# A depthwise 5x5 convolution on TensorE: 24 tiles of up to 128 pixels in the place of 25 squares of 121

## The chip, the core and the metric

The kernel runs on one core of one Trainium2 chip. The metric is the device time of a launch in microseconds (us). Input and output lie in HBM in layouts that the host prepares, and that the kernel may choose.

## What is computed

The input x has 128 images of 55 by 55 pixels with 96 channels, in float32. Each channel is convolved with its own 5 by 5 taps (zero padding, same size), and x is added:

```python
k = jnp.transpose(kernel, (1, 2, 0))[:, :, None, :]
y = lax.conv_general_dilated(x, k, window_strides=(1, 1), padding='SAME', dimension_numbers=('NHWC', 'HWIO', 'NHWC'), feature_group_count=ch)
return x + y
```

## The kernel before

**Tiling.** The 96 channels are taken one after the other. The 55 by 55 plane of a channel is cut into 25 squares of 11 by 11 = 121 pixels. For one square TensorE gets the pixels of all 128 images as its stationary operand (121 pixels on the partitions, 128 images as columns), and as its moving operand a matrix that says to which outputs each pixel contributes: 121 rows, and one column for each output of the 15 by 15 window around the square (at the plane's edges 14 or 13 of a side). The result, 128 images by up to 226 outputs, is summed in PSUM. `x` is split into x_high (rounded to the format that TensorE multiplies in one pass) and x_low (the rest), the taps too, so one square costs three products: x_low by high taps, x_high by high taps, x_high by low taps. Each has its own weight load. That makes 75 products for a channel and 7200 in all (line 428).

**Sums.** Two or three squares that lie under each other share a PSUM bank: 13 sums for a channel, in turn over 8 banks. A sum may begin only when the sum eight before it has been read (`wait_bank`). ScalarE (ACT) copies 10 of the 13 sums to y_out (line 323), VectorE (DVE) copies the other three (354) and adds the seams, four rows (357) or columns (363) wide, in which neighbouring sums overlap.

**Preparing a channel.** x arrives by a DMA of 1.6 MB on SyncE's queue (SP), four channels ahead. ACT makes x_high (315) in two pieces, DVE makes x_low of the first piece, and GpSimd (POOL) x_low of the second (254). POOL also builds the moving operand: `place_taps` (249) multiplies the five turned rows of taps with a mask; the split of the taps for four channels at a time (lines 233, 235, 237) stands in POOL's queue too. weights, x_high and x_low have two slots each, so a channel is prepared while the one before it is multiplied. All queues are written out by hand and each engine takes its own in order.

**Waits.** TensorE (PE) waits for `weights_ready` once a channel, for x_low once a piece, and for the bank of each sum. SP stores a channel (1.5 MB, line 278) when its last seam is added, and behind that store it issues the next load of x.

**Start.** PE first multiplies zeros, 17 products of 512 columns, while the first channel comes in five pieces. The first taps are split and placed by DVE.

Of the kernel before, what the change touches and what calls it, by code (L numbers as in the profile page):

```python
# [14 lines left out]
HALO = TAPS // 2  # L15
P = 128

# [4 lines left out]
SIDE = 11  # L22
GRID = HEIGHT // SIDE
SQUARE = SIDE * SIDE
WINDOW = SIDE + 2 * HALO
SQUARES = GRID * GRID
STRIP_COLS = GRID * IMAGES
X_COLS = SQUARES * IMAGES


TAP_COLS = WINDOW * WINDOW
TAP_AT = 16
PART_COLS = TAP_AT + WINDOW * (WINDOW + 1)
HIGH, LOW = range(2)
# [4 lines left out]
REPEATS = WINDOW // TAPS  # L39
TURNED_COLS = TAPS * WINDOW  # L40
assert WINDOW % TAPS == 0
# [3 lines left out]


EDGE = WINDOW - 1
SUM_COLS = ((1, EDGE),) + ((0, WINDOW),) * (GRID - 2) + ((0, EDGE),)

SEAM = 2 * HALO  # L50
FRESH = tuple(min(WIDTH, SIDE * (j + 1) + HALO) - (SIDE * j + HALO if j else 0) for j in range(GRID))
FRESH_AT = (1,) + (SEAM,) * (GRID - 1)
Y_AT = tuple(HEIGHT * sum(FRESH[:j]) for j in range(GRID + 1))
assert Y_AT[-1] == HEIGHT * WIDTH
Y_COLS = 3072

TILES = tuple((j, squares) for j in range(GRID) for squares in (
    ((0, 1), (2, 3, 4)) if SUM_COLS[j][1] == EDGE else ((0, 1), (2, 3), (4,))))  # L60


def first_row(square):
    return max(0, SIDE * square - HALO)


def end_row(square):
    return min(HEIGHT, SIDE * (square + 1) + HALO)


def tile_rows(tile):
    squares = TILES[tile][1]
    return first_row(squares[0]), end_row(squares[-1])
# [4 lines left out]
def copied_by_act(tile):  # L78
    return len(TILES[tile][1]) > 1


def row_seam(tile):
    return TILES[tile][1][0] > 0


def col_seam(tile):
    return TILES[tile][0] > 0
# [3 lines left out]
COPIES = [sum(copied_by_act(n) for n in range(i + 1)) for i in range(len(TILES))]  # L91
STEPS = [sum((not copied_by_act(n)) + row_seam(n) + col_seam(n) for n in range(i + 1)) for i in range(len(TILES))]
# [5 lines left out]

BATCH = 4
BATCHES = CHANNELS // BATCH  # L100
BATCHES_AHEAD = 2
TAPS_SLOTS = 4
SPLIT_SLOTS = 2
SPLIT_STEPS = 3
ZERO_COLS = 512
ZERO_PRODUCTS = 17


FIRST_PIECES = tuple((j, j + 1) for j in range(GRID))
LATER_PIECES = ((0, 2), (2, GRID))  # L110


def pieces_of(c):
    return FIRST_PIECES if c == 0 else LATER_PIECES

# [6 lines left out]
def uses(c, slots):  # L122

    return c // slots
# [374 lines left out]
```

## Time and profile before

| | |
|---|---|
| median of 3 runs | 821.78 us (820.1 to 821.82) |
| profiled execution: its own time, its span | 820.36 us, 818.6 us |
| PE products; weight loads | 811.2 us busy; 809.2 us |
| ACT, POOL, DVE | 617.4 us (75%), 620.6 us (76%), 538.9 us (66%) |
| DMA | 313.40 MB, mean 383 GB/s |

The span runs from the first to the last instruction. The share of busy time of an engine says how full it is, not whether anything waits for it; for that the chain of waits and the waits of each engine are read. The recorded duration of a product includes its way through the array, so products overlap in the record; their pace is read from the distance between their starts.

### The profile page before, as it was taken

Reading aid. Unit: us, or ns where it says so; the run is one execution under the profiler, and the core shown is the slowest. Engines: PE = TensorE matmul, PEld = TensorE weight load, DVE = VectorE, ACT = ScalarE, POOL = GpSimd, SP = SyncE. Lnnn points to the kernel's source line nnn. Section 1 sums busy time; section 2 is a strip of 40 time slices with the busy share of each in tenths; the row PEclk is TensorE's granted clock in tenths of the full one; section 3 lists DMA queues with packets and bytes.
Section 4 is the critical chain, followed back from the end, with each engine's and each line's share of the span. In section 5 each row is a group of like instructions: output and inputs, shape, how many; then the busy total and the mean of one; then the engine's idle time right before and its main releaser. Section 6 shows DMA issues by size and latency. Waiting matters only on the chain.

```text
span 818.6 us, 19694 instructions
## 1 busy us (share of the span) xinstructions
PE 811.2 (99%) x7217; PEld 809.2 (99%) x7217; DVE 538.9 (66%) x2224; ACT 617.4 (75%) x1157; POOL 620.6 (76%) x263
## 2 busy tenths in 40 slices
PE   8999999999999999999999999999999999999997
PEld 7999999999999999999999999999999999999997
DVE  6666666666666666666666666666666666666664
ACT  6777777777777777777777777777777777777774
POOL 2978878778696786977778878778696786977772
PEclk9999999999999999999999999999999999999999
DMA  9999999999999999999999999999999999999965
GB/s 370 418 414 393 388 387 386 392 385 396 395 389 393 375 402 388 387 391 383 395 391 391 389 386 386 395 381 395 395 387 394 380 399 381 390 390 391 389 246 232
DMA packets 32497, 313.40 MB, mean 383 GB/s; under 512 B 3600, under 2 KB 6800, under 8 KB 8080
## 3 DMA queue, kind: packets, MB, share of 16 engines
q1 hardware_dynamic: 31968, 311.67, 97.4%
q8 instruction: 57, 0.93, 0.4%
q10 hardware_dynamic: 432, 0.46, 0.2%
q14 instruction: 40, 0.33, 0.1%
HBM read 161.13 MB, written 150.99 MB: 381 GB/s over the span
## 4 chain that ended last, share of the span: by engine, by line
PE 98%; DMA 1%; DVE 0%; ACT 0%; ACTq 0%; issue 0%; DVEq 0%
PE sums L428 98%; DMA places_in<-places 1%; DVE x_low L254 0%; DVE weights L249 0%; DVE rest L235 0%; DVE taps_split L233 0%; DVE taps_split L237 0%; ACT y_out L323 0%; ACTq L219 0%; DVEq L163 0%; DVE y_out L357 0%; DVEq L228 0%
## 5 line engine op out<-in xcount | busy, mean ns | idle before, releaser
L428 PE MATMUL sums<-weights,x_high 121*128 121x226 f32 (+3 forms) x4800 | 804.1, 274 | 0.0
L428 PEld LDWEIGHTS sums<-weights,x_high 121*128 121x128 f32 x4800 | 729.0, 192 | 0.0
L428 PE MATMUL sums<-weights,x_low 121*128 121x226 f32 (+3 forms) x2400 | 659.1, 275 | 1.5 <-DVE x_low L254 1.5
L254 POOL TENSOR_TENSOR x_low<-x_in,x_high 121x1920 fp32r<-121x1920 f32 x95 | 411.9, 4336 | 175.3 <-ACT x_high L315 175.3
L323 ACT ACTIVATE y_out<-sums 128x264 f32<-128x264 f32 (+2 forms) x960 | 360.4, 398 | 189.8 <-PE sums L428 176.0
L428 PEld LDWEIGHTS sums<-weights,x_low 121*128 121x128 f32 x2400 | 460.8, 192 | 1.9 <-issue 1.9
L363 DVE TENSOR_TENSOR y_out<-sums,y_out 128x96 f32<-128x96 f32 (+3 forms) x1056 | 263.0, 249 | 123.3 <-ACT y_out L323 102.3
L315 ACT ACTIVATE x_high<-x_in 121x1920 fp32r<-121x1920 f32 (+1 forms) x195 | 295.2, 1514 | 5.3 <-DMA x_in<-x 5.2
L254 DVE TENSOR_TENSOR x_low<-x_in,x_high 121x1280 fp32r<-121x1280 f32 (+1 forms) x100 | 170.1, 1704 | 71.1 <-ACT x_high L315 71.1
L357 DVE TENSOR_TENSOR y_out<-sums,y_out 128x44 f32<-128x44 f32 (+2 forms) x768 | 152.0, 198 | 76.6 <-ACT y_out L323 76.3
L249 POOL TENSOR_TENSOR weights<-taps_split,places_in 121x450 fp32r<-121x450 f32 x95 | 133.7, 1407 | 7.2 <-DVE taps_split L237 7.2
L354 DVE COPY y_out<-sums 128x99 f32<-128x99 f32 x288 | 72.5, 252 | 0.7 <-PE sums L428 0.3
L235 POOL TENSOR_TENSOR rest<-taps_split,places_in 121x300 f32<-121x300 f32 x23 | 43.8, 1905 | 1.8
L237 POOL TENSOR_TENSOR taps_split<-taps_in,rest 121x300 fp32r<-121x300 f32 x23 | 19.3, 838 | 1.8
L233 POOL TENSOR_TENSOR taps_split<-taps_in,places_in 121x300 fp32r<-121x300 f32 x23 | 17.8, 775 | 0.0
L436 PE MATMUL sums<-zeros 128*128 128x512 f32 x17 | 6.9, 588 | 1.5 <-DVE zeros L365 1.5
L436 PEld LDWEIGHTS sums<-zeros 128*128 128x128 f32 x17 | 5.1, 308 | 2.8 <-DVE zeros L365 1.4
L329 ACT ACT_TABLE_LOAD x1 | 1.3, 1283 | 2.1 <-issue 2.1
L233 DVE TENSOR_TENSOR taps_split<-taps_in,places_in 121x300 fp32r<-121x300 f32 x1 | 0.5, 473 | 3.3 <-DMA places_in<-places 3.3
L365 DVE MEMSET zeros<- 128x512 f32 x1 | 0.5, 485 | 0.9 <-PEq L492 0.9
L368 DVE MEMSET weights<- 128x512 f32 x2 | 1.0, 485 | 0.1
L249 DVE TENSOR_TENSOR weights<-taps_split,places_in 121x450 fp32r<-121x450 f32 x1 | 0.6, 628 | 0.0
(9 smaller groups left out, 1.9 us busy)
## 6 DMA issues: line engine op xcount, KB each, us to landing
x_in<-x SPq DMA_DIRECT2D x95, 1600.0 KB, 11.6
y<-y_out SPq DMA_DIRECT2D x95, 1536.0 KB, 7.5
taps_in<-taps SPq DMA_DIRECT2D x22, 150.0 KB, 11.8
x_in<-x SPq DMA_DIRECT2D x5, 320.0 KB, 5.3
y<-y_out SPq DMA_DIRECT2D x3, 302.5 KB, 2.5
y<-y_out SPq DMA_DIRECT2D x1, 357.5 KB, 3.7
taps_in<-taps ACTq DMA_DIRECT2D x2, 150.0 KB, 4.9
y<-y_out SPq DMA_DIRECT2D x1, 271.0 KB, 2.6
```

Source lines behind the costliest of these rows:

```text
L233: engine.tensor_tensor(high, given, centre, ALU.add).then_inc(taps_step, 1)
L235: engine.tensor_tensor(left, high.bitcast(F32), centre, ALU.subtract).then_inc(taps_step, 1)
L237: engine.tensor_tensor(low, given, left, ALU.subtract).then_inc(taps_step, 1)
L249: engine.tensor_tensor(windows, turned, mask, ALU.mult).then_inc(weights_ready[slot], 1)
L254: engine.tensor_tensor(x_low[slot][0:SQUARE, cols], x_in[c % X_SLOTS][0:SQUARE, cols], x_high[slot][0:SQUARE, cols].bitcast(F32), ALU.subt ...
L315: act.activation(x_high[c % SLOTS][0:SQUARE, cols], x_in[c % X_SLOTS][0:SQUARE, cols], ACT.Copy).then_inc(high_ready[c % SLOTS], 1)
L323: act.activation(y, sums, ACT.Copy).then_inc(tile_copied, 1)
L354: dve.tensor_copy(*fresh(c, i)).then_inc(y_step, 1)
L357: dve.tensor_tensor(seam, sums[:, 0:SEAM, FRESH_AT[j]:FRESH_AT[j] + FRESH[j]], seam, ALU.add).then_inc(y_step, 1)
L363: dve.tensor_tensor(seam, sums[:, :, 0:SEAM], seam, ALU.add).then_inc(y_step, 1)
L428: product = pe.matmul(sums, v[slot][0:SQUARE, at:at + IMAGES], window, start=n == 0 and v is x_low, stop=n == len(squares) - 1 and part == ...
L436: pe.matmul(psum[:, 0, :], zeros[:, 0:P], zeros[:, :], start=True, stop=True)
```

## The change

The plane of a channel is cut into 24 tiles: three bands of seven blocks, 16 rows by 8 columns = 128 pixels (the seventh has 7 columns), then a foot of three tiles, 7 rows by 18 columns = 126 pixels. The seven pixels in the last column of the foot are in no tile: their contribution to 9 by 3 outputs is computed on DVE for groups of 12 channels (`sum_corner`, twelve small steps for a group, one in a channel; the first group, of four channels, on POOL before everything else there) and added to the plane of each channel.

A channel has 72 products in 12 sums, 6912 products in all. A window is 12 columns wide and 20 rows high in the second and third band, 18 high in the first; a sum now holds tiles that lie beside each other, so that a product writes rows of 10 or 12 with the pitch of the sum, and no longer one run. x has 3072 columns for a channel (3200 before). y_out is one plane with rows of 55, before it was five strips.

There are two moving operands to place for a channel, for the blocks (128 by 480, one instruction) and for the foot (126 by 225, two instructions), both by POOL. The split of the taps (420 columns for four channels, 300 before) moves from POOL's queue to DVE's, one of its three steps in each of three channels. ACT copies 10 of the 12 sums, DVE two. The first channel comes in other pieces, and DVE makes x_low for three of its five pieces and POOL for two; before, DVE made all. ACT's queue loads 0.55 MB at the start (first taps, centre, mask), 0.12 MB and 1.08 MB (corner), before two taps' batches and 0.15 MB. 14 products of zeros instead of 17.

```diff
+BLOCK_H, BLOCK_W = 16, 8
+BANDS = 3
+STRIPS = 7
+FOOT = BLOCK_H * BANDS
+FOOT_H, FOOT_W = HEIGHT - FOOT, 18
+FOOT_TILES = 3
+FOOT_PIXELS = FOOT_H * FOOT_W
+CORNER_COL = FOOT_W * FOOT_TILES
+assert CORNER_COL == WIDTH - 1
+TILES = BANDS * STRIPS + FOOT_TILES
+X_COLS = TILES * IMAGES
...
+GROUPS = ((0, 4), (4, 12)) + tuple((c, c + 12) for c in range(12, CHANNELS, 12))
+CORNER_STEPS = 2 + 2 * TAPS
...
+SUMS = ((0, (0, 1, 2)), (0, (3, 4)), (0, (5, 6)),
+        (1, (0, 1)), (1, (2, 3)), (1, (4, 5)), (1, (6,)),
+        (2, (0, 1)), (2, (2, 3)), (2, (4, 5)), (2, (6,)),
+        (BANDS, (0, 1, 2)))
...
+def pitch_of(i):
+    first, end = cols_of(i)
+    return end - first + (end - first) % 2
...
+def copied_by_act(i):
+    return i not in (6, 10)
...
-ZERO_PRODUCTS = 17
+ZERO_PRODUCTS = 14
+
+
+FIRST_PIECES = ((0, 3), (3, 7), (7, 14), (14, 21), (21, 24))
+LATER_PIECES = ((0, 11), (11, 24))
...
-    return c == 0 or piece == 0
+    return piece < 3 if c == 0 else piece == 0
...
+        def place_block(engine, c):
+            shape = [P, 2, REPEATS, BLOCK_TURNED]
+            at = c % BATCH * BLOCK_TURNED
+            turned = taps_split[c // BATCH % SPLIT_SLOTS][:, :, at:at + BLOCK_TURNED].bitcast(F32)
+            mask = block_mask.rearrange("p (a n) -> p a n", n=BLOCK_TURNED)
+            windows = block_weights[c % SLOTS][:, :, :].rearrange("p w (a n) -> p w a n", n=BLOCK_TURNED)
+            engine.tensor_tensor(windows, turned.unsqueeze(2).broadcast_to(shape),
+                                 mask.unsqueeze(1).broadcast_to(shape), ALU.mult).then_inc(block_ready[c % SLOTS], 1)
...
+        def place_foot(engine, c):
+            shape = [FOOT_PIXELS, FOOT_ROWS, FOOT_REPEATS, TAPS]
+            at = BATCH * BLOCK_TURNED + c % BATCH * FOOT_TURNED
+            mask = foot_mask[0:FOOT_PIXELS, :].rearrange("p (u b n) -> p u b n", b=FOOT_REPEATS, n=TAPS)
+            for part in (HIGH, LOW):
+                turned = taps_split[c // BATCH % SPLIT_SLOTS][0:FOOT_PIXELS, part, at:at + FOOT_TURNED].bitcast(F32)
+                turned = turned.rearrange("p (u n) -> p u n", n=TAPS).unsqueeze(2).broadcast_to(shape)
+                window = foot_weights[c % SLOTS][0:FOOT_PIXELS, part, :, 0:FOOT_REPEATS * TAPS].rearrange(
+                    "p u (b n) -> p u b n", n=TAPS)
+                engine.tensor_tensor(window, turned, mask, ALU.mult).then_inc(foot_ready[c % SLOTS], 1)
...
+        def sum_corner(engine, group, step):
...
+            engine.wait_ge(corner_step[group > 0], CORNER_STEPS * max(0, group - 1) + step)
+            if step == CORNER_STEPS - 1:
+                own = sums[:, :, HALO:HALO + FOOT_H, HALO]
+                engine.tensor_tensor(own, pixels, own, ALU.add).then_inc(corner_step[group > 0], 1)
+                return
...
+            if adds:
+                to = sums[:, :, row:end_row, :]
+                engine.tensor_tensor(to, part, to, ALU.add).then_inc(corner_step[group > 0], 1)
+            else:
...
+                engine.tensor_tensor(part, pixels[:, :, row + shift:end_row + shift].unsqueeze(3).broadcast_to(shape),
+                                     rows.unsqueeze(2).broadcast_to(shape), ALU.mult).then_inc(corner_step[group > 0], 1)
...
-            load_taps(act, 0)
-            act.dma_start(places_in[:, :], places).then_inc(places_loaded, 16)
+            act.dma_start(start_in[:, :], start).then_inc(start_loaded, 16)
+            act.dma_start(foot_mask[:, :], foot).then_inc(foot_loaded, 16)
+            act.dma_start(corner_in[:, :], corner).then_inc(corner_loaded, 16)
...
+                if col_seam(i):
+                    seam = y[:, row + down:end_row, col:col + SEAM]
+                    dve.tensor_tensor(seam, sums[:, down:, 0:SEAM], seam, ALU.add).then_inc(y_step, 1)
+                if i == LAST_SUM:
+                    dve.wait_ge(y_step, stepped(c, i) - 1)
+                    group = group_of(c)
+                    dve.wait_ge(corner_step[group > 0], CORNER_STEPS * max(1, group))
+                    part = corner_sum[group % GROUP_SLOTS][:, c - GROUPS[group][0], :, :]
+                    seam = y[:, HEIGHT - CORNER_ROWS:HEIGHT, WIDTH - CORNER_OUT:WIDTH]
+                    dve.tensor_tensor(seam, part, seam, ALU.add).then_inc(y_step, 1)
 
...
+                todo = []
+                group = group_of(c)
+                first, end = GROUPS[group]
+                if group + 1 < len(GROUPS):
+                    share = [CORNER_STEPS * (n - first) // (end - first) for n in (c, c + 1)]
+                    todo = list(range(*share))
+                if c // BATCH + 1 < BATCHES and c % BATCH < SPLIT_STEPS:
+                    split_taps(dve, c // BATCH + 1, c % BATCH)
...
+                    if i in (5, 8, 11) and todo:
+                        sum_corner(dve, group + 1, todo.pop(0))
...
-            for c in range(1, CHANNELS):
-                place_taps(pool, c)
-                split_low(pool, c, 1, low_by_pool)
-                if c % BATCH == BATCH // 2 and c // BATCH + 1 < BATCHES:
-                    split_taps(pool, c // BATCH + 1)
+            pool.wait_ge(start_loaded, 16)
+            pool.wait_ge(corner_loaded, 16)
+            for step in range(CORNER_STEPS):
+                sum_corner(pool, 0, step)
+            pool.wait_ge(foot_loaded, 16)
+            for c in range(CHANNELS):
+                wait_split(pool, c)
+                if c > 0:
+                    place_block(pool, c)
+                place_foot(pool, c)
+                for piece in range(len(pieces_of(c))):
+                    if not by_dve(c, piece):
+                        split_low(pool, c, piece, low_by_pool)
 
...
+                    sums = sum_view(c, i)[:, :, to:to + right - left]
+                        if foot_tile:
+                            window = foot_weights[slot][0:pixels, part, :, left:right]
...
+                            window = block_weights[slot][:, part, :].rearrange("p (r c) -> p r c", c=WINDOW_W)[
+                                :, above:above + end - first, left:right]
```

What stands in the queues, at three places.

POOL in the middle of the program before: one batch of four channels (`weights` is the moving operand, `rest` and `taps_split` the split of the taps).

```order
L249 TENSOR_TENSOR weights<-taps_split,places_in 121x2x225
L254 TENSOR_TENSOR x_low<-x_in,x_high 121x1920
L233 TENSOR_TENSOR taps_split<-taps_in,places_in 121x4x75
L235 TENSOR_TENSOR rest<-taps_split,places_in 121x300
L237 TENSOR_TENSOR taps_split<-taps_in,rest 121x4x75
L249 TENSOR_TENSOR weights<-taps_split,places_in 121x2x225
```

POOL at its beginning now (from the last steps of the corner to the second channel; `foot_weights` and `block_weights` are the two moving operands).

```order
L347 TENSOR_TENSOR corner_part<-corner_in 128x84
L341 TENSOR_TENSOR corner_sum0<-corner_part,corner_sum0 128x4x21
L332 TENSOR_TENSOR corner_sum0<-corner_in,corner_sum0 128x4x7
L306 TENSOR_TENSOR foot_weights0<-taps_split0,foot_mask 126x9x25 x2
L311 TENSOR_TENSOR x_low0<-x_in0,x_high0 128x896
L311 TENSOR_TENSOR x_low0<-x_in0,x_high0 128x384
L294 TENSOR_TENSOR block_weights1<-taps_split0,start_in 128x480
L306 TENSOR_TENSOR foot_weights1<-taps_split0,foot_mask 126x9x25 x2
L311 TENSOR_TENSOR x_low1<-x_in1,x_high1 128x1664
```

The split of the taps has left POOL; the corner of the first group now stands ahead of x_low of the first channel, and each later channel is one block, two feet and one x_low.

DVE now, in the first part of a channel in the middle (the step at line 280 is the third of a split, that at 347 a step of the corner; 448 and 453 are the seams).

```order
L311 TENSOR_TENSOR x_low<-x_in,x_high 128x1408
L280 TENSOR_TENSOR taps_split<-taps_in,rest 128x420
L448 TENSOR_TENSOR y_out<-sums,y_out 128x18x4 x2
L453 TENSOR_TENSOR y_out<-sums,y_out 128x4x18
L448 TENSOR_TENSOR y_out<-sums,y_out 128x16x4
L453 TENSOR_TENSOR y_out<-sums,y_out 128x4x20
L448 TENSOR_TENSOR y_out<-sums,y_out 128x16x4
L453 TENSOR_TENSOR y_out<-sums,y_out 128x4x20
L347 TENSOR_TENSOR corner_part<-corner_in 128x252
L445 COPY y_out<-sums 128x16x5
```

Before, the same stretch had no split and no corner:

```order
L254 TENSOR_TENSOR x_low<-x_in,x_high 121x1280
L357 TENSOR_TENSOR y_out<-sums,y_out 128x52
L363 TENSOR_TENSOR y_out<-sums,y_out 128x24x4
L357 TENSOR_TENSOR y_out<-sums,y_out 128x44
L363 TENSOR_TENSOR y_out<-sums,y_out 128x26x4
L354 COPY y_out<-sums 128x99
```

A step of the split (in three channels of four) now stands between x_low and the seams, and a step of the corner between them.

PE before, three squares inside the plane (121 rows by 226 outputs in one run), and now, three blocks of the second band (20 rows of 12 outputs, with the pitch of the sum).

```order
L428 MATMUL sums<-weights,x_low 128x226
L428 MATMUL sums<-weights,x_high 128x226 x2
L428 MATMUL sums<-weights,x_low 128x226
L428 MATMUL sums<-weights,x_high 128x226 x2
L428 MATMUL sums<-weights,x_low 128x196
```

```order
L542 MATMUL sums<-block_weights,x_low 128x20x12
L542 MATMUL sums<-block_weights,x_high 128x20x12 x2
L542 MATMUL sums<-block_weights,x_low 128x20x12
L542 MATMUL sums<-block_weights,x_high 128x20x12 x2
L542 MATMUL sums<-block_weights,x_low 128x200
```

A tile keeps its three products; a product has up to 240 columns where it had up to 226.

## Rows read from the trace of the kernel before

**Rows 1.** The page, part 1: engine, busy us (share of the span) xinstructions.
```profile
PE 811.2 (99%) x7217; PEld 809.2 (99%) x7217; DVE 538.9 (66%) x2224; ACT 617.4 (75%) x1157; POOL 620.6 (76%) x263
```

**Rows 2.** Chain of work that ended last: start us, us, what.
```profile
1.17 4.73 DMA places_in<-places
...
5.98 0.48 DVE taps_split L233
...
7.50 0.63 DVE weights L249
8.13 1.59 DVE x_low L254
9.72 0.14 issue
9.85 804.28 PE sums L428 x7200
```

**Rows 3.** Timeline of PE mid-program: start us, us, instruction.
```profile
403.58 0.27 PE L428 MATMUL sums<-weights,x_low 121*128 121x182 f32 x1
...
403.92 0.29 PE L428 MATMUL sums<-weights,x_low 121*128 121x210 f32 x1
...
405.26 0.27 PE L428 MATMUL sums<-weights,x_low 121*128 121x196 f32 x1
...
405.59 0.28 PE L428 MATMUL sums<-weights,x_low 121*128 121x226 f32 x1
...
405.94 0.27 PE L428 MATMUL sums<-weights,x_low 121*128 121x226 f32 x1
```

**Rows 4.** Timeline of PE's zero products: all, the last three, the last two.
```profile
1.45 6.90 PE L436 MATMUL sums<-zeros 128*128 128x512 f32 x17 [1.45 <-DVE zeros L365]
...
7.49 0.86 PE L436 MATMUL sums<-zeros 128*128 128x512 f32 x3
...
7.72 0.63 PE L436 MATMUL sums<-zeros 128*128 128x512 f32 x2
```

**Rows 5.** Groups by form: count | busy us, mean ns | idle before, releaser.
```profile
L254 POOL TENSOR_TENSOR x_low<-x_in,x_high 121x1920 fp32r<-121x1920 f32 x95 | 411.9, 4336 | 175.3 <-ACT x_high L315 175.3
...
L249 POOL TENSOR_TENSOR weights<-taps_split,places_in 121x450 fp32r<-121x450 f32 x95 | 133.7, 1407 | 7.2 <-DVE taps_split L237 7.2
...
L323 ACT ACTIVATE y_out<-sums 128x242 f32<-128x242 f32 x288 | 108.0, 375 | 52.8 <-PE sums L428 52.8
...
L323 ACT ACTIVATE y_out<-sums 128x403 f32<-128x403 f32 x96 | 49.0, 510 | 0.6 <-PE sums L428 0.6
L235 POOL TENSOR_TENSOR rest<-taps_split,places_in 121x300 f32<-121x300 f32 x23 | 43.8, 1905 | 1.8
...
L237 POOL TENSOR_TENSOR taps_split<-taps_in,rest 121x300 fp32r<-121x300 f32 x23 | 19.3, 838 | 1.8
```

**Rows 6.** POOL's instructions of line 249: ns min/median/max, first and last start.
```profile
L249 POOL TENSOR_TENSOR weights<-taps_split,places_in x95: 1034/1092/2422, 7.6 to 798.5; 121x450 fp32r<-121x450 f32 x95
```

**Rows 7.** Groups by form of ACT's and DVE's other work, as rows 5.
```profile
L315 ACT ACTIVATE x_high<-x_in 121x1920 fp32r<-121x1920 f32 x95 | 171.1, 1801 | 0.0
L254 DVE TENSOR_TENSOR x_low<-x_in,x_high 121x1280 fp32r<-121x1280 f32 x95 | 165.5, 1742 | 71.1 <-ACT x_high L315 71.1
...
L357 DVE TENSOR_TENSOR y_out<-sums,y_out 128x44 f32<-128x44 f32 x576 | 113.9, 198 | 1.5 <-ACT y_out L323 1.2
...
L363 DVE TENSOR_TENSOR y_out<-sums,y_out 128x96 f32<-128x96 f32 x384 | 100.0, 260 | 123.3 <-ACT y_out L323 102.3 <-DVE y_out L357 0.5
```

**Rows 8.** Windows: us, busy of each engine (x), granted clock, DMA share, GB/s.
```profile
36.00:56.00 20.00, 20.00 (x182) 20.00 (x181) 13.37 (x51) 15.71 (x30) 14.05 (x6) 1.00 1.01 424
400.00:420.00 20.00, 20.00 (x181) 20.00 (x180) 13.10 (x59) 14.98 (x30) 15.84 (x7) 1.00 1.00 381
420.00:440.00 20.00, 20.00 (x182) 20.00 (x180) 12.88 (x50) 15.46 (x29) 16.88 (x9) 1.00 1.00 396
...
816.00:818.00 2.00, 0.00 (x0) 0.00 (x0) 0.00 (x0) 0.00 (x0) 0.00 (x0) 0.58 0.72 277
```

**Rows 9.** DMA issues: count, KB each, median us to landing.
```profile
x_in<-x SPq DMA_DIRECT2D x95, 1600.0 KB, 11.6
```

More of the change, by code:

```diff
@@ L93, with row_seam, col_seam @@
+def copied_by_act(i):
+    return i not in (6, 10)
+def row_seam(i):
+    return SUMS[i][0] > 0
+def col_seam(i):
+    return SUMS[i][1][0] > 0
+LAST_SUM = len(SUMS) - 1
+COPIES = [sum(copied_by_act(n) for n in range(i + 1)) for i in range(len(SUMS))]
+STEPS = [sum((not copied_by_act(n)) + row_seam(n) + col_seam(n) + (n == LAST_SUM) for n in range(i + 1))
+         for i in range(len(SUMS))]
 COPIES_ALL, STEPS_ALL = COPIES[-1], STEPS[-1]
@@ L152, in bank_of, with group_of, build @@
 def bank_of(c, i):
-    return (c * len(TILES) + i) % BANKS
-LAST_TILE = len(TILES) - 1
+    return (c * len(SUMS) + i) % BANKS
+def group_of(c):
+    return next(g for g, (first, end) in enumerate(GROUPS) if first <= c < end)
 LAST = CHANNELS - 1
-LAST_STORES = tuple((Y_AT[j], Y_AT[j + 1] if j < GRID - 1 else Y_COLS) for j in range(GRID))
-def build(nc, x, taps, places, out):
+LAST_STORES = ((6, 0, WIDTH * (2 * BLOCK_H - HALO)),
+               (10, WIDTH * (2 * BLOCK_H - HALO), WIDTH * (FOOT - HALO)),
+               (11, WIDTH * (FOOT - HALO), Y_COLS))
+def build(nc, x, taps, start, foot, corner, out):
     with ExitStack() as ctx:
@@ L443, in _ @@
                     pe.wait_ge(low_ready[slot], lows(c, piece))
[L444 to L446 removed]
+                    for i in range(len(SUMS)):
+                        if first <= tiles_of(i)[0] < end:
+                            sum_tiles(c, i)
 def lay_out_input(x):
[L450 to L451 removed]
@@ new lines, in lay_out_masks, with lay_out_corner @@
+def lay_out_masks():
+    block = np.zeros((P, WINDOW_H, WINDOW_W), np.float32)
+    for r in range(BLOCK_H):
+        block[r * BLOCK_W:(r + 1) * BLOCK_W, r:r + TAPS] = 1
+    foot = np.zeros((P, FOOT_ROWS, FOOT_REPEATS * TAPS), np.float32)
+    for c in range(FOOT_W):
+        foot[c:FOOT_PIXELS:FOOT_W, :, c:c + TAPS] = 1
+    return block.reshape(P, -1), foot.reshape(P, -1)
+def lay_out_corner(x, taps):
+    pixels = x[:, FOOT:, CORNER_COL, :].transpose(0, 2, 1).reshape(P, -1)
+    reach = taps[:, :, :HALO - 1:-1].reshape(1, -1)
+    return np.concatenate([pixels, np.repeat(reach, P, axis=0)], axis=1)
```

378 lines of the change are left out of this document (191 added, 187 removed).

## The prediction

> **What bounds the kernel now.** I read the page's shares of busy time first: PE and its weight loads stand at 99%, ACT, POOL and DVE at 66 to 76% [rows 1]. A busy share alone doesn't say that an engine sets the end, so the chain of waits comes next. It is one piece: 804.28 us of products in a row, from 9.85 on, no wait between them [rows 2]. Only the start (9.85 us) and the tail (818.6 - 814.1 = 4.5 us) lie outside. So the question is what sets the pace of a product: 804.28 / 7200 = 111.7 ns.
>
> The timeline answers it. A product of x_low begins a tile of three. From 403.58 to 403.92 (182 columns) are 0.34 us, from 403.92 to 405.26 (nine products of 210 columns, three of 182) 1.34 us or 111.7 ns each, from 405.26 to 405.59 (196) 0.33 us, from 405.59 to 405.94 (226) 0.35 us [rows 3]. At 2.4 GHz a column takes 0.417 ns, so 182 columns would need 76 ns and 226 94 ns: the pace follows the products and not their columns. What every product has alike is one load of 128 weight columns. A load has 268 cycles of 2.4 GHz here. PE is therefore bound by the number of products, and columns are free as long as a product streams in less than 111.7 ns.
>
> **What the change does, part by part.**
>
> *Products.* 75 become 72 for a channel, 7200 become 6912: 6912 x 111.7 = 772.1 us, 32.2 less. Columns rise from 15,594 to 15,648 for a channel, which costs nothing by the pace above. One form is new in size: 240 columns, in five tiles of each of two bands, 30 products a channel, 2880 in all. They stream in 100 ns, 11.7 under the pace. Bounds: from below nothing is gained (the load stays). From above the last zero products have 512 columns and start 0.23 us apart, where 213 ns are 512 columns, so some 17 to 20 ns lie between two long products [rows 4]; a product of 240 columns would take up to 120 ns, 8.3 more, 24 us in all. I take nothing: with 20 ns on top, the 2592 products of 226 columns would need 114 ns and the mean of all products would be 112.6, not the 111.7 that the stretch of 210 columns has. But 226 leaves 17.5 ns free and 240 only 11.7, and the writes to PSUM now go in rows of 10 or 12, so I keep the 24 us.
>
> The stationary operand has 128 rows of pixels instead of 121. The trace has no paced load of 128 rows: the nearest is the load of 121 rows. If the time went by rows, it were 111.7 x 128/121 = 118.2 ns. The 268 cycles are 2.09 for each of 128 columns, near a whole number, and 2.21 for each row; I take no change. The Trainium skill (TensorE: Matmul & The Clock Gate, section LDWEIGHTS (loading the stationary operand)) says that a load takes P/1.2 ns with P the columns, whatever the rows: 106.7 ns for 128. By that rule the term stays 772, by rows it would be 815; the trace has 5 ns more than the rule.
>
> *POOL, for each channel.* x_low of 13 tiles is 1664 columns where 1920 took 4336 ns, 2.26 ns each [rows 5]: 3.76 us. The block window is 480 columns; 450 took 1407 ns on average, 3.13 each, but 1034 in the fastest and 2422 in the slowest [rows 6]: 1.50 us (1.1 to 2.6). The foot is 2 x 225 columns in runs of five. No row has such runs; the nearest by size are 838 ns for 300 columns (2.8 each) and 1905 for 300 (6.35 each) [rows 5]: 1.26 us, up to 2.86. The sum is 6.5 us, between 6.1 and 9.2, against 72 x 111.7 = 8.04 us in which PE now does a channel. POOL's share rises from 76 to some 81% though the split of the taps leaves it. What counts is when x_low of the second piece is there: PE wants it after 11 tiles, 3.7 us into the channel, and waits for nothing as long as POOL's channel is under 8.04 us. That leaves 8.04 - 3.76 = 4.28 us for 930 columns, 4.6 ns each. I stay with the cheaper rows.
>
> *ACT.* Ten copies stay ten; their columns rise from 2728 to 2865. 242 columns take 375 ns and 403 take 510 [rows 5], 0.84 ns a column: 0.1 us more. x_high loses 128 columns of 3200, 0.1 us less [rows 7]. ACT keeps its 6.4 us a channel, 80% of 8.04.
>
> *DVE.* 538.9 / 96 = 5.6 us a channel now [rows 1]. x_low grows from 1280 to 1408 columns, by a tenth of 1742 ns [rows 7]: 0.2. A channel has 18 seams and two copies, and one corner add, for 22 operations before, about the same (198 to 260 ns each, overlapping [rows 7]). The split adds 0.6 us in three of four channels, a corner step some 0.4 to 0.5 us in each: 0.9 on average. Sum 6.6 us, 82% of 8.04. Behind these steps the seams of a channel are queued, and for them PE's bank waits: a sum wants the bank of the one eight before, 5.4 us earlier. x_high and x_low of the next channel come first (3.7 us from the channel's start), then the split and the seams of the first five sums, to about 5.2 us; the first such bank is wanted at 6.0. It is close and I count nothing; without that cover it costs tenths of a us a channel.
>
> *DMA.* A channel moved 1.64 + 1.57 + 0.04 = 3.25 MB in 8.38 us, 388 GB/s. Now it is 1.57 + 1.57 + 0.05 = 3.20 MB in 8.04 us, 398 GB/s. The DMA share is 1.00 throughout, at 381 to 396 GB/s; but for 20 us, right after the start, the same mix ran at 424 [rows 8], and a load lands after 11.6 us [rows 9] of the three channels (25 us) it has. So 398 is within reach. The Trainium skill (HBM Reference, section Specifications (TRN2)) gives a core 358 GB/s as its share when both cores of the domain run, and some 425 to one alone; by the first figure 309 MB would take 862 us, and the trace is already above it (383 on average).
>
> *Start.* Before, PE begins at 9.85: taps and mask land 4.73 us after their issue, three splits of 0.48, placing 0.63, x_low 1.59 [rows 2]. Now 0.55 MB has to land for 0.31 (0.6 us at 424 GB/s), the splits have 420 columns for 300 (0.5 in all), the first piece of x_low 384 for 640 (0.5 less): 10.4. Then POOL. It waits for 1.08 MB of the corner, behind 0.67 MB on ACT's queue and beside 1.6 MB of x: 3.3 MB at 424 GB/s are 7.8 us, there at about 10. The corner has 904 columns, 2.5 to 5.7 us at 2.8 to 6.35 ns; the feet 1.3 to 2.9; x_low of 896 columns 2.0. PE wants that after 42 products, at 15.1, and it is there at 15.8 to 20.6: 0.7 to 5.5 us of waiting, I take 3. PE's clock: the first 14 zero products took 6.04 us or 431 ns each, which is 1.2 GHz, and the next 0.23 [rows 4]; after the last product at 814.1 the granted clock is 0.58 in the window from 816 on [rows 8]. With three zero products fewer PE idles from 7.6 to 10.4, and again in the wait for POOL. Another slow stretch like the first costs half of its 6 us: I take 3, with bounds 0 and 6.
>
> *Tail.* As before, plus one add for the corner: 4.8 us.
>
> **Sum.** 10.4 + 772.1 + 3 + 3 + 4.8 = 793.3 us of span. The profiled execution's own time is 820.36 for a span of 818.6, 1.8 more; the median of the runs is 821.78, another 1.4: 796.5, say **797 us**. With the start's bounds alone 791 to 803.
>
> **The rivals.**
> (a) *POOL becomes the bound, and the kernel slower.* If the short runs of the foot and the block window cost what the slow rows cost (6.35 and 5.4 ns a column), POOL's channel is 3.76 + 2.6 + 2.86 + 0.15 for gaps = 9.4 us; 95 x 9.4 + 22 for the first channel + 8 for the end and the difference of times = 923 us. It decides from 4.6 ns a column on. For it: the slow rows exist (a mean of 1407 over a median of 1092 means that about one placing in four is slow [rows 6]), and these windows have more and shorter runs. Against: the median placing is 1092 ns, 2.4 a column. With slow feet alone POOL takes 8.3 us and the time is about 818.
> (b) *The wide products set their own pace*, 120 ns: 797 + 24 = 821, in a weaker form 809.
> (c) *The DMA is at its end at 388 GB/s*, as its share of 1.00 says: 3.20 MB take 8.24 us a channel, 95 x 8.24 + 30 = 813. Against it stands the 424.
> (d) *Loads go by rows*: 815.4 in place of 772.1, 840 us.
> (e) *The seams come late for the banks* on DVE's longer queue: 0.1 us a channel, 807.
>
> **Chances.** The forecast 0.58; (a) 0.10 in full and 0.05 in half; (b) 0.13; (c) 0.07; (d) 0.03; (e) 0.04. About 0.2% (1.6 us) is what a measurement of this kernel tells from no change. Faster: 0.58 and the half of (a), most of (b), (c) and (e), 0.84; same: the upper end of (b), 0.03; slower: (a) in full and (d), 0.13. The range reaches from 786 (no waits at the start, no slow clock, a shorter tail) to 820; it leaves out (a), (d) and a bit of the rest.
>
> **What would show it.** Right: the 6912 products take 111.7 ns each also where they have 240 columns; PE waits once for x_low by POOL before 22 us and hardly after. Wrong: starts 118 to 120 ns apart in the second and third band (b) or everywhere (d); waits of PE for POOL's x_low in every channel, with feet over 1.3 us each (a); ACT waiting for x to land and loads landing after 20 us or more (c); waits of PE for DVE's seams (e).

## The result, and the profile after

The changed kernel took **854.38 us** (median of 4 runs, 853.85 to 856.42) against 821.06 of the kernel before in the same job: a ratio of 1.0411, with a 95% interval of 1.0389 to 1.0433. It is slower; 797 was forecast. The profiled execution has a span of 852.9 us, where the sum of the prediction was 793.3.

The page's part 1 of the kernel after, columns as in [rows 1]:

```profile
PE 806.1 (95%) x6926; PEld 789.8 (93%) x6926; DVE 780.4 (91%) x2193; ACT 613.9 (72%) x1157; POOL 635.1 (74%) x400
```

PE lost its 99%. DVE went from 538.9 to 780.4 us, 2.5 us more a channel where I had 1.0, with fewer instructions than before (2193 for 2224). So something on DVE became long. The groups by form (count | busy us, mean ns of one | idle before, releaser) say what:

```profile
L347 DVE TENSOR_TENSOR corner_part<-corner_in 128x252 f32<-128x252 f32 x21 | 66.4, 3163 | 0.0
L341 DVE TENSOR_TENSOR corner_sum<-corner_part,corner_sum 128x252 f32<-128x252 f32 x21 | 64.9, 3091 | 0.0
...
L332 DVE TENSOR_TENSOR corner_sum<-corner_in,corner_sum 128x84 f32<-128x84 f32 x7 | 20.7, 2951 | 0.0
```

A corner step of 252 columns takes 3.1 us, and one of 84 columns nearly as long: the time isn't made of columns. The timeline (start us, us, instruction) shows what it is made of; two stretches of DVE, then the one of POOL beside the second:

```profile
37.09 0.30 DVE L347 TENSOR_TENSOR corner_part<-corner_in 128x144 f32<-128x144 f32 x1
...
402.79 0.23 DVE L453 TENSOR_TENSOR y_out<-sums,y_out 128x80 f32<-128x80 f32 x1
402.94 3.52 DVE L347 TENSOR_TENSOR corner_part<-corner_in 128x252 f32<-128x252 f32 x1
406.38 0.23 DVE L445 COPY y_out<-sums 128x80 f32<-128x80 f32 x1
...
402.41 3.77 POOL L311 TENSOR_TENSOR x_low<-x_in,x_high 128x1664 fp32r<-128x1664 f32 x1 [2.42 <-ACT x_high L406]
```

POOL's x_low runs from 402.41 to 406.18. DVE's corner step begins 0.5 us after it and ends at 406.46, 0.28 us after it. The seam just ahead of it, at 402.79, also lies beside x_low and takes its 0.23 us. The step at 37.09, with POOL idle, takes 0.30. So the step does no work for 3.2 us: it stands still until POOL is done. It is the rule and not the exception: of the 88 steps on DVE, 76 begin while POOL's x_low runs, and each of them ends 0.14 to 0.29 us behind it. Every seam behind such a step in DVE's queue stands too, and PE, which wants the banks that the seams read, waits for them. PE's waits (us in total, times, longest):

```profile
PE sums L542 <- DVE y_out L453: 30.0, 75, 0.5
PE sums L542 <- POOL x_low L311: 4.8, 1, 4.8
PE sums L542 <- DVE y_out L448: 4.2, 1, 4.2
PE sums L542 <- DVE x_low L311: 2.6, 2, 2.0
```

What else the prediction asked of the profile is there as forecast. The groups of POOL by form:

```profile
L311 POOL TENSOR_TENSOR x_low<-x_in,x_high 128x1664 fp32r<-128x1664 f32 x95 | 358.8, 3777 | 191.1 <-ACT x_high L406 190.4
...
L306 POOL TENSOR_TENSOR foot_weights<-taps_split,foot_mask 126x225 fp32r<-126x225 f32 x192 | 148.4, 794 | 0.0
L294 POOL TENSOR_TENSOR block_weights<-taps_split,start_in 128x480 fp32r<-128x480 f32 x95 | 127.1, 1338 | 5.0 <-PE sums L542 5.0
```

x_low 3.78 us (3.76 forecast), a foot 0.79 (0.63), the blocks 1.34 (1.50): 6.7 us a channel, far from rival (a). The last twelve channels have no corner steps, and there, from 753.88 us on, PE is never idle. Windows, columns as in [rows 8]:

```profile
400.00:420.00 20.00, 19.11 (x168) 18.75 (x168) 19.11 (x50) 14.99 (x28) 12.76 (x9) 1.00 0.96 367
...
780.00:800.00 20.00, 20.00 (x181) 20.00 (x180) 16.66 (x59) 15.85 (x31) 19.27 (x11) 1.00 1.01 423
```

From 753.88 us on 849 products start within 95.04 us, 112.1 ns apart; products of 240 columns are among them and start 0.34 us apart by threes like the others. That refutes rival (b), wide products, and (d), loads by rows. The DMA moves 423 GB/s there, which refutes (c). The 367 GB/s of the middle are what a slower channel asks for, not a limit.

### The profile page after: what moved, and what is told of

The parts are those of the page before. It is cut to its first block, busy times and chain, and to the rows that moved or that the text cites. A ratio compares the mean times of both kernels' runs of the same rounds, so it can differ in the third digit from the quotient of the medians.

```text
span 852.9 us, 19211 instructions
## 1 busy us (share of the span) xinstructions
PE 806.1 (95%) x6926; PEld 789.8 (93%) x6926; DVE 780.4 (91%) x2193; ACT 613.9 (72%) x1157; POOL 635.1 (74%) x400
## 2 busy tenths in 40 slices
DMA packets 32351, 309.93 MB, mean 363 GB/s; under 512 B 3584, under 2 KB 6912, under 8 KB 7808
## 4 chain that ended last, share of the span: by engine, by line
DVE 52%; PE 38%; issue 3%; ACT 3%; DMA 1%; POOL 1%; SPq 0%; DVEq 0%; ACTq 0%
PE sums L542 38%; DVE corner_sum L341 13%; DVE corner_part L347 11%; DVE x_low L311 9%; DVE y_out L453 7%; DVE y_out L448 5%; DVE corner_sum L332 2%; ACT y_out L414 2%; DVE y_out L445 2%; DMA x_in<-x 1%; ACT x_high L406 1%; DVE taps_split L280 1%; DVE rest L277 1%; DVE y_out L460 1%; DVE taps_split L274 1%
## 5 line engine op out<-in xcount | busy, mean ns | idle before, releaser
L542 PE MATMUL sums<-block_weights,x_high 128*128 128x240 f32 (+3 forms) x4032 | 691.6, 276 | 0.0
L542 PEld LDWEIGHTS sums<-block_weights,x_high 128*128 128x128 f32 x4032 | 613.3, 192 | 0.0
L542 PE MATMUL sums<-block_weights,x_low 128*128 128x240 f32 (+3 forms) x2016 | 565.8, 281 | 41.6 <-DVE y_out L453 30.0
L414 ACT ACTIVATE y_out<-sums 128x256 f32<-128x256 f32 (+3 forms) x960 | 368.0, 418 | 224.8 <-PE sums L542 224.6
L311 POOL TENSOR_TENSOR x_low<-x_in,x_high 128x1664 fp32r<-128x1664 f32 (+1 forms) x97 | 363.3, 3745 | 191.1 <-ACT x_high L406 190.4
L542 PEld LDWEIGHTS sums<-block_weights,x_low 128*128 128x128 f32 x2016 | 386.4, 192 | 56.8 <-DVE y_out L453 43.5
L406 ACT ACTIVATE x_high<-x_in 128x1664 fp32r<-128x1664 f32 (+1 forms) x195 | 284.2, 1458 | 7.8 <-DMA x_in<-x 7.8
L453 DVE TENSOR_TENSOR y_out<-sums,y_out 128x80 f32<-128x80 f32 (+3 forms) x864 | 206.8, 239 | 38.2 <-ACT y_out L414 9.5
L311 DVE TENSOR_TENSOR x_low<-x_in,x_high 128x1408 fp32r<-128x1408 f32 (+2 forms) x98 | 169.9, 1734 | 11.7 <-ACT x_high L406 11.7
L448 DVE TENSOR_TENSOR y_out<-sums,y_out 128x64 f32<-128x64 f32 (+1 forms) x768 | 160.2, 219 | 11.5 <-ACT y_out L414 9.0
L347 DVE TENSOR_TENSOR corner_part<-corner_in 128x252 f32<-128x252 f32 (+5 forms) x40 | 122.7, 3067 | 0.0
L341 DVE TENSOR_TENSOR corner_sum<-corner_part,corner_sum 128x252 f32<-128x252 f32 (+5 forms) x40 | 111.7, 2792 | 0.0
L460 DVE TENSOR_TENSOR y_out<-corner_sum,y_out 128x27 f32<-128x27 f32 x96 | 25.2, 262 | 3.3
```

The source lines that it names most:

```text
L311: engine.tensor_tensor(x_low[slot][:, cols], x_in[c % X_SLOTS][:, cols], x_high[slot][:, cols].bitcast(F32), ALU.subtract).then_inc(low_re ...
L341: engine.tensor_tensor(to, part, to, ALU.add).then_inc(corner_step[group > 0], 1)
L347: engine.tensor_tensor(part, pixels[:, :, row + shift:end_row + shift].unsqueeze(3).broadcast_to(shape), rows.unsqueeze(2).broadcast_to(sh ...
L406: act.activation(x_high[c % SLOTS][:, cols], x_in[c % X_SLOTS][:, cols], ACT.Copy).then_inc(high_ready[c % SLOTS], 1)
L414: act.activation(y, sums, ACT.Copy).then_inc(tile_copied, 1)
L448: dve.tensor_tensor(seam, sums[:, down:, 0:SEAM], seam, ALU.add).then_inc(y_step, 1)
```

## The experiments

Each ratio is to the kernel before in the same job, which had 820.2 to 822.0 us. "Period" is the mean time from a channel's first product to the next channel's, over channels 8 to 80; before it is 8.375 us, after 8.671, and 72 products at 111.7 ns would be 8.04. "Start" is the same for channels 0 to 2 together: 25.2 before, 40.8 after.

**Is it the corner at all?** *no_corner* takes the steps and the corner's add out; its output lacks the seven pixels' contributions. *memset_steps* leaves them in their places, but from the second group on each is a memset of what it would write; the corner's values are then zeros.

```diff
-                    if i in (5, 8, 11) and todo:
-                        sum_corner(dve, group + 1, todo.pop(0))
...
```
```diff
...
+            if group:
+                engine.memset(sums[:, :, row:end_row, :] if adds else part, 0.0).then_inc(corner_step[1], 1)
```

> The changed kernel without anything of the corner: no steps of it on DVE or POOL, and no add of it (seven pixels' contributions are left out). Theory W (DVE's corner steps, two inputs from SBUF each, stand still while POOL's x_low of 3.8 us runs, and hold up the seams and so PE's banks): PE hardly waits after the start, a channel takes 8.04 us, and with the start's wait for POOL shorter the time is 787 to 796. Rival R (DVE's queue is too long with the split of the taps and x_low even without the corner, or the DMA is at its end): a channel stays above 8.3 us, 815 or more.

> The changed kernel with every corner step after the first group replaced by a memset of the same output, in the same place on DVE (no inputs; the corner's values from channel 4 on are left out). Theory W: a memset has no input from SBUF and does not wait for POOL: 0.3 us each, a channel of 8.04 us, 792 to 806. Rival P (any instruction on DVE in that place, or writing SBUF beside POOL, is held up, or the mere place in the queue costs): 3 us each and 845 to 860.

Measured 797.35 us for no_corner (ratio 0.971, interval 0.9688 to 0.9733; 1.4 us above its range) and 797.35 for memset_steps (0.9712, 0.9692 to 0.9732). Both have a period of 8.061. The corner costs 57 us, and all of it goes when the instructions stay in place, in number and in output, and write a constant in the place of reading SBUF and adding or multiplying. A memset of 252 columns takes:

```profile
L343 DVE MEMSET corner_part<- 128x252 f32 x21 | 5.6, 268 | 0.0
```

So it isn't the number of instructions in the queue, nor a semaphore, nor the write.

**The same thing made in the kernel before.** *probe_in_before* puts one add of 252 columns from two SBUF tensors behind the seams of sum 5 of each channel; *probe_copy* a copy of 252 columns; *probe_reduce* a sum of neighbours (252 columns read, 126 written).

```diff
...
+                    if i == 5:
+                        dve.wait_ge(probe_step, 2 + c)
+                        dve.tensor_tensor(probe[0][:, :], probe[1][:, :], probe[2][:, :], ALU.add).then_inc(probe_step, 1)
```

> The kernel before with one more instruction a channel: DVE adds two SBUF tensors of 252 contiguous columns (a probe that nothing uses) behind the seams of the sixth sum, where POOL's x_low of 4.34 us runs. Theory W (a DVE operation with two inputs from SBUF stands still until POOL's x_low ends): the add takes 2.5 to 4 us instead of 0.4, DVE's 5.6 us a channel grow to 8.5 to 9.5 against 8.38, PE waits for seams, and the time is 850 to 920. Rival Q (the changed kernel's DVE is only too full, its steps slow by their strides): 0.4 us, and 820 to 824.

> The kernel before with one more DVE instruction a channel, in the place of probe_in_before's 252-column add: a copy of as many columns from SBUF to SBUF, one input, float32. Theory (only an instruction of DVE with two SBUF inputs stands still beside POOL's x_low): the copy takes 0.2 to 0.4 us and the kernel 820 to 824. Rival (DVE's instruction stops by whatever it does in SBUF, or a one-input copy takes POOL's port as well): the copy takes 3 to 4 us, ends with POOL's x_low, and the kernel comes to 900 to 950, like probe_in_before (951.9).

> The kernel before with one DVE instruction more a channel, in the place of probe_copy's copy: it reads the same 252 columns from SBUF and writes the 126 sums of two neighbours. By the Trainium skill (SBUF - State Buffer, section Who interferes with whom) a copy between SBUF tensors can take POOL's pair of ports, a reduction on this chip never does. Theory (the DVE instruction stops only if it needs POOL's ports, by a second SBUF input or as a copy that reads through both): the reduction takes 0.2 to 0.5 us and the kernel 820 to 824. Rival (any DVE instruction whose inputs are all in SBUF stops): it takes 3 to 4 us and the kernel 930 to 950, like probe_copy (938.9).

Measured 951.85 us (ratio 1.1595, 1.1573 to 1.1616), 938.9 (1.1421, 1.1392 to 1.145) and 820.61 (1.0001, 0.999 to 1.0012). The groups of the three probes, one of each kernel:

```profile
L388 DVE TENSOR_TENSOR probe<-probe 128x252 f32<-128x252 f32 x96 | 384.2, 4002 | 0.0
```
```profile
L388 DVE COPY probe<-probe 128x252 f32<-128x252 f32 x96 | 370.6, 3860 | 0.0
```
```profile
L388 DVE TENSOR_REDUCE probe<-probe 128x126 f32<-128x252 f32 x96 | 38.9, 406 | 0.0
```

One small add a channel costs this kernel 131 us, more than the 30 to 100 that I expected; 95 of the 96 adds end 0.27 to 0.28 us behind POOL's x_low, and the one that doesn't meet it takes 0.41 us. My own theory for the copy (only two inputs stop) was refuted: a copy stops as well, 95 of the 96, and ends 0.15 us behind x_low (0.28 us where it meets none). The reduction, with its input in SBUF too, doesn't; it lies inside POOL's x_low in the timeline and takes 0.41 us:

```profile
362.28 0.41 DVE L388 TENSOR_REDUCE probe<-probe 128x126 f32<-128x252 f32 x1
...
361.88 4.33 POOL L256 TENSOR_TENSOR x_low<-x_in,x_high 121x1920 fp32r<-121x1920 f32 x1 [3.00 <-ACT x_high L317]
```

This is the rule of the Trainium skill (SBUF — State Buffer, section Who interferes with whom): DVE and POOL share one pair of SBUF ports, and it is a lock held for a whole instruction, not a bandwidth. DVE needs it for a second SBUF input or when a copy reads through both ports; a reduction on this chip never does. By that rule and these runs seams (one input in PSUM) and memsets are free, as the trace has them.

**Where the steps stand.** *corner_early* puts them behind the split of the taps, before a channel's first seam; *corner_late* behind its last seam; *corner_on_pool* gives them to POOL, behind its x_low.

```diff
                 for i in range(len(SUMS)):
                     finish_sums(c, i)
-                    if i in (5, 8, 11) and todo:
-                        sum_corner(dve, group + 1, todo.pop(0))
+                for step in todo:
+                    sum_corner(dve, group + 1, step)
```

> The changed kernel with the same corner steps on DVE, only placed directly behind the split of the taps at the channel's beginning, before the first seam, where POOL waits for x_high. Theory W: a step takes about 0.3 us instead of 3.1, a channel 8.04 us, the time is 790 to 803 (the start stays as it is, 10 to 15 us of loss). Rival S (the steps are slow by themselves, by runs of three elements and strides): they take 3 us here too, and the time stays at 845 to 860.

> The changed kernel with the corner steps of a channel on DVE behind its last seam, where DVE waits 0.9 us a channel for x_high in the run without a corner, and POOL places the block. Theory W extended (V: DVE's and POOL's instructions with two SBUF inputs share one supply, their times add up, and with the corner it is POOL whose channel passes 8.04 us): steps of 0.3 to 0.9 us, POOL's channel 8.1 to 8.25 us as in the early placing, 803 to 820. If only x_low's standing still counted (W alone): 795 to 802.

> The changed kernel with all later corner steps moved from DVE to POOL, behind its x_low of the channel. Theory W: POOL takes 0.6 to 0.9 us for a step of 252 columns, its channel rises from 6.4 to some 7.2 us, under 8.04; DVE's seams are no longer held up; 792 to 806. Rival S: slow runs cost on POOL too (3 us), POOL's channel passes 9 us, 870 or more.

Measured:

| kernel | us, ratio (interval) | period | start | a 252-column step (L347) |
|---|---|---|---|---|
| corner_early | 819.1, 0.9984 (0.9972 to 0.9996) | 8.149 | 40.7 | 0.86 us |
| corner_late | 809.66, 0.9853 (0.9814 to 0.9892) | 8.150 | 40.6 | 1.12 us |
| corner_on_pool | 823.28, 1.0027 (1.0016 to 1.0039) | 8.336 | 34.4 | 0.70 us, on POOL |

The diff is that of corner_late. The same instructions, moved in one queue, win back 45 us there: none of the 88 begins beside x_low, they meet POOL's blocks and feet (0.6 to 1.3 us long). corner_early's trace is 21.3 us longer than no_corner's: 9.7 of it lie in the start, 5.7 in channel 5, which took 13.7 us because a step of 3.80 us just met x_low and held the seams, and some 7 are spread over the others. That expectation (790 to 803) was missed, and so was corner_on_pool's (792 to 806). On POOL a step costs no more than it does beside short instructions, but POOL is now busy for 97% of the span (94% in no_corner), its own standing counted: its block takes 2.30 us on average where it takes 1.23 in no_corner. PE waits 36 times for DVE's seams, 10.1 us in all. corner_late's time is inside its range (803 to 820). DVE and then POOL, two stretches of one timeline of corner_on_pool:

```profile
355.67 1.52 DVE L460 TENSOR_TENSOR y_out<-corner_sum,y_out 128x27 f32<-128x27 f32 x1
357.11 2.09 DVE L311 TENSOR_TENSOR x_low<-x_in,x_high 128x1408 fp32r<-128x1408 f32 x1
359.13 1.61 DVE L274 TENSOR_TENSOR taps_split<-taps_in,start_in 128x420 fp32r<-128x420 f32 x1
...
357.09 0.64 POOL L341 TENSOR_TENSOR corner_sum<-corner_part,corner_sum 128x216 f32<-128x216 f32 x1
357.67 2.62 POOL L294 TENSOR_TENSOR block_weights<-taps_split,start_in 128x480 fp32r<-128x480 f32 x1
360.25 1.62 POOL L306 TENSOR_TENSOR foot_weights<-taps_split,foot_mask 126x225 fp32r<-126x225 f32 x2
```

The shortest records of their forms are 1.61 and 0.59 us for DVE's x_low and split, 1.21 and 2 x 0.62 for POOL's block and feet, 4.7 in all, and with POOL's step ahead of them (0.64) some 5.3; side by side they needed 4.8 (357.09 to 361.87). So in this stretch about nine tenths of their times add up as if the two were one engine. The corner's add of 27 columns, with two inputs in SBUF as well, takes 1.52 us beside POOL's x_low, and 0.19 where it meets nothing.

**More work from POOL to DVE.** *late_dve14* is corner_late with 14 tiles of x_low on DVE; *late_dve14_start* also moves the first group's steps from POOL to DVE.

```diff
-LATER_PIECES = ((0, 11), (11, 24))
+LATER_PIECES = ((0, 14), (14, 24))
```

> As corner_late, and the boundary between DVE's and POOL's x_low moves from tile 11 to tile 14: DVE takes 1792 columns, POOL 1280. Theory V: a column costs DVE 1.15 ns and POOL 2.26, so the shared supply is used 0.43 us less a channel and POOL's channel falls to some 7.3 us: PE hardly waits after the start, 790 to 803. If DVE's length is what counts (its channel grows by 0.44 us to 6.8 or more): 815 to 830.

> As late_dve14, and the corner of the first group is computed by DVE behind its pieces of x_low of channel 0, no longer by POOL ahead of everything. Theory V: POOL starts x_low of channel 0 some 5 us earlier, PE's wait of 4.8 us near 14 us goes, with it most of the slow clock behind it: 5 to 12 us less than late_dve14, 784 to 795. If the start is bound by the landing of x: no difference.

Measured 812.26 us (0.9894, 0.9879 to 0.9909; period 8.206) and 813.43 (0.991, 0.9896 to 0.9925), both missed. POOL's share fell to 71% and DVE's rose to 91%, yet the channel got 0.06 us longer. My theory had the sum of both engines' SBUF work as the bound, and by its prices that sum fell by 0.43 us a channel (384 columns, 2.26 - 1.15 ns each). So the sum alone doesn't set the pace here. POOL sat idle for 215 us before its x_low, for want of x_high; the few waits that PE's rows show from 60 to 780 us (4, 1.1 us in all) are for DVE's seams. DVE's in-order queue is then the likelier bound, but no run separates the two. The start of late_dve14 is shorter, 35.2 us for the 40.6 of corner_late.

**One late step.** *start_and_balanced* is start_reordered (below) with a group's corner steps collected in every fourth channel, where no taps are split.

> start_reordered with the corner steps of a group of four channels put into its fourth channel alone, where no taps are split (in group 0 three steps a channel). Theory: the lost time of 0.09 us a channel of corner_late is the corner steps and the taps' split together in one channel of DVE; apart, the period comes to 8.07 to 8.10 us, 4 to 6 us less than start_reordered: 791 to 799. Rival (what is lost is each corner step's time beside POOL, wherever it stands): the mean period stays at 8.13 to 8.16 and the time within 2 us of start_reordered; or four times as many steps in one channel fill it past 8.05 us and the period is above 8.16.

Measured 926.62 us (four runs, 918.07 to 936.39; the ratio, 1.1238, interval 1.1171 to 1.1306, is that of the three up to 929.32), 128 us above the upper end of its range. The trace is of the execution of 936.39. DVE, then POOL:

```profile
134.59 0.42 DVE L347 TENSOR_TENSOR corner_part<-corner_in 128x252 f32<-128x252 f32 x1
135.04 0.42 DVE L341 TENSOR_TENSOR corner_sum<-corner_part,corner_sum 128x252 f32<-128x252 f32 x1
135.50 0.30 DVE L332 TENSOR_TENSOR corner_sum<-corner_in,corner_sum 128x84 f32<-128x84 f32 x1
135.70 1.63 DVE L311 TENSOR_TENSOR x_low<-x_in,x_high 128x1408 fp32r<-128x1408 f32 x1
137.23 4.09 DVE L274 TENSOR_TENSOR taps_split<-taps_in,start_in 128x420 fp32r<-128x420 f32 x1
...
135.79 5.08 POOL L311 TENSOR_TENSOR x_low<-x_in,x_high 128x1664 fp32r<-128x1664 f32 x1 [1.53 <-ACT x_high L408]
```

The steps make DVE's x_low late, it meets POOL's x_low, and now POOL is the one that waits (5.08 us for 3.77); the split behind it then waits for POOL (4.09 for 0.59), and PE waits 5.4 us for the seams. Whichever starts first holds the ports. PE waited so 22 times, 81.9 us in all, and most of these channels took 14 to 15 us. The granted clock adds to it: 1.00 from 120 to 135 us and 0.77 from 135 to 150, where PE waited 5.4.

**The start.** *start_reordered* is corner_late with ACT's copies and DVE's first seams of channel 0 before x_high and x_low of channel 1, the first group's corner steps on DVE before channel 0's last seam, and the corner's load on SP's queue. *corner_inside_start* has these steps between the seams of sums 3 and 4, the second group's in channels 1 to 3, and the corner's load on ACT's queue behind the second taps. The diff, against the changed kernel, is of the latter:

```diff
...
+                early = range(5) if c == 0 else ()
+                for i in early:
+                    finish_sums(c, i)
+                    if i == 3:
+                        dve.wait_ge(corner_loaded, 16)
+                        for step in range(CORNER_STEPS):
+                            sum_corner(dve, 0, step)
...
```

> Corner steps behind the last seam of a channel, as in corner_late (809.7 us), and the first channels reordered: ACT copies channel 0's sums before it makes x_high(1), DVE adds the seams of channel 0's sums 0 to 4 before it makes x_low(1), the first group's corner steps stand on DVE just before the last sum's seam, and POOL starts with the feet. Theory (DVE's and POOL's instructions with two SBUF inputs stop each other, and the queue behind them is what PE waits for): the periods of channels 8 to 95 stay at 8.13 to 8.16 us, and of the start's 9 us beyond 8.05 in channel 0 and some 6 in channel 1 some 8 to 12 come back: 797 to 803. Rival (the start's loss is the first loads from HBM and the cold clock, not the order of DVE, ACT and POOL): channel 0 keeps 16 to 17 us and the time stays at 808 to 811.

> start_reordered with the first group's corner steps between the seams of channel 0's sums 3 and 4, where DVE waits for x_high of channel 1 (10.7 to 16.1 us), and the second group's in channels 1 to 3. Theory (in start_reordered corner steps beside POOL's x_low of channel 2 held the seams until 31 us, a wait of 5.7 us for PE and then a slow clock until 41 us): channels 0 to 2 take 27 to 32 us together where they took 40.6, and the kernel 797 to 802. Rival (the start costs the same wherever the corner steps stand, by the loads from HBM or the clock): 38 to 41 us and 808 to 811.

Measured 810.1 us (0.986, 0.9832 to 0.9889) and 807.24 (0.9868, 0.981 to 0.9927; its runs reach from 804.5 to 815.4, so the two are not told apart by their times). The traces tell more. In start_reordered channel 0 fell from 17.1 to 9.7 us, but channel 1 rose from 14.4 to 20.6: two of the first group's steps met x_low (3.7 and 3.6 us), PE waited 5.7 us, and the granted clock of 31.4 to 39.4 was 0.50, which is 1.2 GHz, where 14 to 22 had 1.00. The forecast of 797 to 803 was missed: the time is the rival's (808 to 811), though channel 0 fell as the theory had it. In corner_inside_start channels 0 to 2 take 32.4 us in place of 40.6, just outside the 27 to 32 expected, and the period stays at 8.142; its time, too, lies above the expected 797 to 802. Its PE waits:

```profile
PE sums L553 <- DVE x_low L311: 6.6, 2, 3.7
PE sums L561 <- DVE zeros L464: 1.5, 1, 1.5
PE sums L553 <- DVE y_out L450: 1.1, 5, 0.3
```

corner_late, start_reordered and corner_inside_start are the fastest complete kernels of this study, 1.3 to 1.5% faster than before and not told apart from each other. Above no_corner, the traces of the first and the last have 7.9 and 7.5 us from channel 3 on, some 0.08 us a channel, and 9.5 and 1.3 in the start.

## Why the prediction was wrong

The predicted span was 793.3 and the measured one 852.9, 59.6 us more. By the steps of the prediction:

- **Products: right.** 112.1 ns each where nothing waits (8.061 / 72 = 112.0 in no_corner), 240 columns and 128 rows included: 0.3 ns above the 111.7 of the sum, 2 us in all.
- **POOL: right** in its rows (6.7 us a channel, 6.5 forecast), and in no_corner and memset_steps PE waits for it nowhere behind the first channel. But rival (a) priced it by rows that were themselves waits, as told below.
- **ACT, DMA: right.** ACT 6.4 us a channel; 423 GB/s reached when asked for.
- **DVE: the step that failed.** "a corner step some 0.4 to 0.5 us": the price holds for a step that meets nobody (0.30 us for 144 columns, 0.42 for 252 in start_and_balanced), but beside x_low it takes 3.1. The overlap was wrong: a step on DVE and POOL's x_low were taken to run side by side, and they don't. "It is close and I count nothing; without that cover it costs tenths of a us a channel": this cover was not there. From channel 3 to the end of the last product the trace after has 799.8 us, where 93 channels of 8.04 are 747.9: 51.9 us of the 59.6. In memset_steps the same stretch has 749.9, so 49.9 of the 51.9 are the steps' standing and 2.0 the pace of the products. The symptom had been named as rival (e), seams late for the banks, at 0.1 us a channel and a chance of 0.04; it took 0.6 in the middle channels (8.671 - 8.04). The stop behind it had not been named: the nearest rows were those of the seams [rows 7], whose one input lies in PSUM. No row of before showed a short instruction with two SBUF inputs on DVE beside POOL's x_low. memset_steps shows that the cost lies in what the step reads and computes and not in its place, number or writes; probe_in_before and the ends of its adds behind x_low show the standing still without the rest of the change. (The count of seams was off as well, 17 a channel and not 18, which changes nothing.)
- **The start: mis-sized, for the most part by the same step.** Channels 0 to 2 took 40.8 us, for 24.1 of products and 6 of waits and slow clock allowed: 10.7 more. PE waited 4.8 us for x_low by POOL, inside the 0.7 to 5.5 given, and 4.2 more for seams behind the taps' split, which itself stood 4.1 us beside POOL's x_low; then the clock was 0.76 in 20 to 40 us. The split met x_low because a corner step ahead of it had stood 3.89 us (from 24.15 on): in memset_steps the split is done before POOL's x_low begins, the wait of 4.2 us is gone, and the start takes 33.5 us. So 7.3 of the 10.7 are the corner's too, and 3.4 remain. First product at 8.57 for 10.4 (1.8 less), and a tail of 3.7 for 4.8 (1.1 less). 51.9 + 10.7 - 1.8 - 1.1 = 59.7.

The corner step, the split and POOL's x_low beside the split, in the start of the changed kernel:

```profile
24.15 3.89 DVE L347 TENSOR_TENSOR corner_part<-corner_in 128x120 f32<-128x120 f32 x1
...
31.91 4.08 DVE L277 TENSOR_TENSOR rest<-taps_split,start_in 128x420 f32<-128x420 f32 x1
...
31.66 3.88 POOL L311 TENSOR_TENSOR x_low<-x_in,x_high 128x1664 fp32r<-128x1664 f32 x1 [1.35 <-ACT x_high L406]
```

The trace of before had a sign that I read wrongly. POOL's line 249 had 1034 ns at least and 2422 at most [rows 6], and I took the long ones for a matter of runs in memory. They are those that lie beside DVE's x_low. All 24 of over 2.3 us share 1.39 to 1.46 us with it, and the other 71 took up to 1.1 us (one 1.4). One of the 24, and DVE's x_low beside it:

```profile
405.42 2.42 POOL L249 TENSOR_TENSOR weights<-taps_split,places_in 121x450 fp32r<-121x450 f32 x1
...
405.38 1.49 DVE L254 TENSOR_TENSOR x_low<-x_in,x_high 121x1280 fp32r<-121x1280 f32 x1 [0.74 <-ACT x_high L315]
```

Here DVE began first and took 1.49 us; where POOL's placing began half a us earlier, it is DVE's x_low that took 1.9, which makes its mean of 1742 [rows 7]. The 1905 ns of `rest` on POOL [rows 5], from which rival (a) had its upper price for the feet, are of the same kind: each of the 23 shares 1.27 us with DVE's x_low. So the 923 us of rival (a) rested on waits and not on short runs, and the same rows told of the stop that made the kernel slower.

## What to carry to other kernels

Before adding a DVE instruction ask where its inputs lie and what POOL does in that stretch: if both inputs are in SBUF, or it is an SBUF to SBUF copy, price it as what is left of POOL's instruction, and the queue behind it too. A minimum and a maximum far apart for one form, on DVE or POOL, is how a trace shows this before it hurts. Where both engines do SBUF-to-SBUF work of this kind (reductions and memsets on DVE aside), expect most of their times to add up; but moving work between them until the sum falls isn't enough, as late_dve14 shows. Put DVE's short instructions beside POOL's short ones.

## What the runs showed of the hardware

The stop works both ways: DVE's step waited 3.2 us for POOL, and POOL's x_low took 5.08 us instead of 3.77 behind DVE's. An SBUF to SBUF copy waits like an add of two inputs (3.86 and 4.00 us for 252 columns beside x_low, 0.28 and 0.41 without it), a reduction does not (0.41 beside it). In start_reordered a wait of PE of 5.7 us was followed by a granted clock of 0.50 over 31.4 to 39.4 us and 0.62 over 39.4 to 45.0. 65 products started in these 13.6 us, for which 7.3 would do at 112.1 ns; 1.3 us of the rest were another wait. By this estimate the clock cost 5 us more, nearly the length of the wait again.
